# A shorter ring of per-expert buffers: six epack buffers become four in the routed expert stage

## What is computed

```python
x = _layernorm(x + attn(x))
aff = x @ centroids.T
assign = argmax(aff); alpha = sigmoid(aff of the chosen expert)
for e in range(8):                       # y of each token by its own expert alone
    h = relu(_layernorm(xs, ln_g[e], ln_b[e]) @ w1[e].T + b1[e])
    ye = xs + h @ w2[e].T + b2[e]
out = alpha * y + (1 - alpha) * xs
x = _layernorm(x + out)
```

## Time and profile before

| | |
|---|---|
| median of three runs | 863.51 us |
| profiled execution | 863.51 us, span 861.7 us |
| TensorE busy in the span | 837.3 us (97%) |
| VectorE, ScalarE, GpSimd busy | 456.1, 354.5, 282.1 us |
| mean granted TensorE clock | 0.994 |
| chain that ended last | TensorE 85%, VectorE 7%, DMA 2%, SyncE's stream 2% |
| moved by DMA | 93.29 MB, mean 108 GB/s |

### The profile page before, as it was taken

One profiled execution on the slowest core, in us unless ns is written; L12 is line 12 of the kernel. 1 busy time (PEld: TensorE's weight loads), 2 busy tenths in 40 slices (PEclk: granted clock), 3 DMA queues, 4 the chain that ended last, 5 costly groups with the idle time before them and its releaser, 6 DMA issues.

```text
span 861.7 us, 19429 instructions
## 1 busy us (share of the span) xinstructions
PE 837.3 (97%) x7394; PEld 559.6 (65%) x7394; DVE 456.1 (53%) x1334; ACT 354.5 (41%) x591; POOL 282.1 (33%) x392
## 2 busy tenths in 40 slices
PE   8999999999999999999999999999999899999994
PEld 5545576477466557557547646769988676767673
DVE  5465355256256346445528625624687465555552
ACT  1443425523532531631542453323232467565660
POOL 3503021422152060152142225224554444444422
PEclk9999999999999999999999999999999999999998
DMA  6501100020020020010003103333544897988830
GB/s 246 184 2 30 46 2 1 26 75 1 26 75 1 26 74 2 26 41 34 2 27 123 32 19 102 134 135 121 178 151 136 297 344 273 319 303 286 294 121 15
DMA packets 38594, 93.29 MB, mean 108 GB/s; under 512 B 13988, under 2 KB 26917, under 8 KB 30567
## 3 DMA queue, kind: packets, MB, share of 16 engines
q1 hardware_dynamic: 33206, 80.42, 26.4%
q0 software_dynamic: 4864, 11.10, 4.3%
q10 hardware_dynamic: 432, 0.54, 0.2%
HBM read 81.07 MB, written 11.23 MB: 107 GB/s over the span
## 4 chain that ended last, share of the span: by engine, by line
PE 85%; DVE 7%; DMA 2%; issue 2%; SPq 2%; ACT 1%; another core or an unknown queue 0%; POOL 0%; DVEq 0%; POOLq 0%; ACTq 0%
PE ps L598 13%; PE ps L604 12%; PE ps L545 9%; PE ps L569 7%; PE ps L691 7%; PE ps L709 6%; PE ps L731 4%; PE ps L755 4%; PE ps L517 3%; PE ps L577 3%; PE ps L444 3%; PE ps L465 3%; PE ps L473 3%; PE ps L407 2%; DMA wts<-in_w 1%
## 5 line engine op out<-in xcount | busy, mean ns | idle before, releaser
L604 PE MATMUL ps<-ff2T,hT 128*128 128x256 f32 x512 | 121.0, 384 | 0.2 <-ACT hT L1523 0.2
L598 PE MATMUL ps<-x3x,ff1T 128*128 128x512 f32 x256 | 118.8, 604 | 0.1
L1531 ACT ACTIVATE arena<-ps 128x1536 f32<-128x1536 f32 (+3 forms) x49 | 65.1, 1328 | 128.3 <-DVE arena L998 127.8
L604 PEld LDWEIGHTS ps<-ff2T,hT 128*128 128x128 f32 x512 | 94.3, 190 | 16.3 <-issue 3.4
L998 DVE SCALAR_TENSOR_TENSOR arena<-ps,arena 128x512 f32<-128x512 f32 (+4 forms) x59 | 44.9, 767 | 106.4 <-PE ps L545 64.0
L709 PE MATMUL ps<-w_sb,arena 128*128 x400 | 95.6, 382 | 0.0
L709 PEld LDWEIGHTS ps<-w_sb,arena 128*128 128x128 f32 x400 | 72.2, 190 | 16.0 <-issue 8.2
L598 PEld LDWEIGHTS ps<-x3x,ff1T 128*128 128x128 f32 x256 | 45.6, 190 | 52.2 <-issue 49.9
L545 PE MATMUL ps<-arena 32*128 32x512 f32 (+7 forms) x896 | 73.0, 434 | 1.8 <-ACT hT L1017 1.2
L545 PEld LDWEIGHTS ps<-arena 32*128 32x128 f32 x896 | 36.0, 184 | 37.2 <-issue 31.0
L1523 ACT ACTIVATE hT<-ps,col 128x512 f32<-128x512 f32 x64 | 43.8, 685 | 35.7 <-PE ps L598 35.1
(11 more groups left out here) (231 smaller groups left out, 1584.7 us busy)
## 6 DMA issues: line engine op xcount, KB each, us to landing
arena<-in_w SPq DMA_DIRECT2D x27, 1024.0 KB
hT<-in_w SPq DMA_DIRECT2D x16, 1024.0 KB
wts<-in_w SPq DMA_DIRECT2D x9, 1024.0 KB
w_sb<-in_w SPq DMA_DIRECT2D x8, 1024.0 KB, 5.1
token_store<-x SPq DMA_DIRECT2D x8, 520.0 KB, 3.7
arena<-in_x SPq DMA_DIRECT2D x8, 512.0 KB, 3.8
arena<-in_epack SPq DMA_DIRECT2D x18, 134.0 KB
slot_table<-padid POOLq DMA_DIRECT2D x4, 576.0 KB
```

The lines of the kernel that those rows point to most:

```text
L598: last = eng.matmul(ps[:, 6 + m % 2, :], ff1T[:, kd, m * P:(m + 1) * P], xT3[:, kd, :], start=kd == 0, stop=kd == KD - 1)
L604: last = eng.matmul(quarter(6, t), hT[:, m, t * P:(t + 1) * P], ff2T[:, m, :], start=m == 0, stop=m == FM - 1)
L1531: eng.activation(o, i, ACT.Relu).then_inc(s_sa, 1)
```

## The change

EN becomes 4. The tensor `ep_more` goes, all four buffers are those in the arena, and the four epack loads ahead of the loop are counted by EN instead of WN (both are 4). The wait in `slot_sp_ep` is not edited, but its index changes with EN: it now names the tile four before instead of six.

```diff
-UN, WN, XN, EN = 3, 4, 6, 6
+UN, WN, XN, EN = 3, 4, 6, 4
...
-        ep_more = sb("ep_more", [P, 2, EW + 12 * (NP - 1)])
...
-        ep = ring(at, EW + 12 * (NP - 1), EN - 2) + [ep_more[:, u, :] for u in range(2)]
-        at += (EN - 2) * (EW + 12 * (NP - 1))
+        ep = ring(at, EW + 12 * (NP - 1), EN)
+        at += EN * (EW + 12 * (NP - 1))
...
-                    for j in range(WN):
+                    for j in range(EN):
                         slot_sp_ep(eng, j, slot_sp_rows(eng, j))
```

## The result

The changed kernel takes 884.0 us (median of 4 runs, 883.1 to 886.4) against 863.6 for the kernel before on the same chip: ratio 1.0245, 95% interval 1.0219 to 1.0271, 20 us slower. The profiled execution took 882.1 us, with a span of 879.9.

What follows compares the result with a forecast made beforehand. TensorE, busy 147.6 of 150 us in the expert stage, was taken as the bound, with SyncE's load queue nearly late. Tile 14's 1.9, mixed tiles' 14.7 and tile 32's 1.5 sum to 18.1; 863.5+18.1 = 881.6, stated as 881, range 868 to 893.

Steps and rivals of the forecast that it cites:

- One of my own signs of being wrong: Whole run: the prediction is wrong if the granted clock falls more than once or twice more.
- Where the wait binds: SyncE's epack loads: tile j now waits for y(j-4); tiles 13, 21 and 28 go 1.8 to 8.0 us later.
- Tiles 4 to 12, nothing: Full tiles with one weight block each: weights and ids still arrive in time, so no cost.
- Tile 14, +1.9: Tile 13's held epack delays tile 14's blocks; TensorE's 2.37 us stall becomes 4.3, half clock already paid.
- The loop: Mixed tiles, y(j-4) to y(j-2): reaction 0.2, issues 5.7, ids 9.8, gather to y 3.1; 18.8 us, longer than two tiles.
- the 14.7: Mixed tiles: loop excesses 5.1, 7.6 and 6.2 us, less 1.4 hidden per run, leave 3.7+6.2+4.8 = 14.7.
- the hidden time: VectorE's lag: 1.4 us costs nothing, once per run of mixed tiles, until TensorE's turn at line 741.
- Tile 32, +1.5: Last mixed tile, no ids behind it: weights come 16.9 us after y28, wanted after 15.4, so +1.5 us.
- Rival (a): Ids overtake the weights, only the weights loop is left: 871.0 us; chance 0.14.
- (b): Rival, hidden: bursts land faster, loop below 16 us, only part of tile 14 costs: 863.5 to 865; chance 0.07.
- (c): Rival, faster: held SyncE clears the queue ahead of tile 14, stall and half clock go: 859.3 us; chance 0.04.
- (d): Rival: every new stall also halves the clock, 1.8 us each for eight more tiles, 881+14 = 895; chance 0.10.

Runs made afterwards that it cites:

- mixed-only run: Kernel before, six buffers, with the epack's wait for y(j-4) only at the nine mixed tiles, y(j-6) at full tiles: 880.3 us, ratio 1.0206.
- full-only run: Kernel before, six buffers, with the epack's wait for y(j-4) only at the full tiles, y(j-6) at mixed tiles: ratio 1.0040.
- second set: The second of three sets of follow-up measurements; the kernel before had a median of 860.1 us in it.
- five-buffer kernel: Kernel before with EN = 5, one of the two buffers in ep_more left unused: ratio 0.9998.
- ids experiment: Changed kernel, four buffers; from tile 14 on SyncE issues the ids of tile j+3 ahead of tile j's epack and weights: 870.7 us, ratio 1.0092.

## Why the prediction was right

**Forecast 881 us, measured 884.0.** The profiled execution took 882.1 against my sum of 881.6. That the two are so near is partly luck: several terms were off and cancelled, as below. One of my own signs of being wrong came too: I allowed the granted clock to fall once or twice more, and it falls three times more.

**Where the wait binds**: right. From tile 4 on the epack leaves 0.2 us after y(j-4), except where SyncE is later: at 22 of 30 tiles. I wrote some twenty such waits; eighteen are in the view.

**Tiles 4 to 12, nothing**: right, within 0.2 us up to y11.

**Tile 14, +1.9**: right by its size (y13 is 2.0 late, gap 4.10 for the 4.3 forecast) and its cause: the gap is gone but for 0.73 us in the mixed-only run, whose time is 4 us lower, and alone in the full-only run. Inside it two errors cancelled. The third block left 3.9 us later (676.07 for 672.16, since SyncE issued the blocks more slowly too), not 1.9, and TensorE started on it 9.3 us after its issue, not 11.3. The step took the half clock as paid already. That held in the traces compared; on the chip of the second set the five-buffer kernel had none, and tile 14 cost 3.5.

**The loop**: right. 18.8 forecast; 18.6, 18.5 and 18.7 measured at tiles 21, 23 and 25. Its terms were 0.2, 5.7, 9.8 and 3.1, and at tile 21 they are 0.2, 6.3, 9.0 and 3.1, so two were off by 0.6 and 0.8 in opposite senses; over all seven turns they are 6.3 and 9.2 on the mean. The ids experiment shows that this loop and not the weights carries the loss, though the gaps in the view stand at the weights: what ends a gap last is not what set its length. The excess of the loop, from y12 to y16, y17 to y23 and y24 to y28, was 5.3, 7.0 and 6.3 us for the 5.1, 7.6 and 6.2 forecast. But the runs of mixed tiles cost 5.0, 5.1 and 5.2 for 3.7, 6.2 and 4.8, so what was hidden or won back was 0.3, 1.9 and 1.1 us, not 1.4 each time. That the sum, 15.3, comes near to the 14.7 is luck in this part. Nor does TensorE stand where I had the hidden time end: at the transposes of the rows (line 741) it waits 0.3 us; what it stands more is at layer 1.

**Tile 32, +1.5**: 0.9 measured.

**Rival (a)**, ids overtaking the weights: fell. Ids issued behind three blocks started their gather 9.0 us later at tile 21, and 8.1 to 10.0 at all seven. **(b)** fell: no turn of the loop took under 18.5 us, for its 16. **(c)** fell: tile 14's gap grew. **(d)**, the clock halving at each stall: in part. The granted clock drops behind tiles 14, 18, 23 and 30, and TensorE is busy 4.6 us more, for the 14 that it named. Yet the time of the loop forecast holds without a term for it. That a slower TensorE inside a loop of SyncE, DMA, GpSimd and VectorE only fills time it would have stood is my reading; no run took the clock away.

## What to carry to other kernels

A ring's length isn't only a question of whether its own tiles arrive in time. Where one queue issues everything in order, the wait for a free buffer holds all that follows, so close the loop by hand: from the event waited for through every load behind it back to that event, against the time that the ring leaves; below it costs nothing, above it costs the excess at each turn (none at five buffers, 2.5% at four, 18% for a wait three tiles back). If such a wait must be shortened, move the large, early loads ahead of it first, and keep a small load that an engine needs soon off the back of a burst.

## What the runs showed of the hardware

TensorE's clock behind a gap of about two microseconds can go either way. At tile 14 it stood 2.37 us and its next matmuls took 1.08 us (1.2 GHz), and in another kernel, with the same work up to there, it stood 2.05 us and they took 0.63 (2.4 GHz); behind 3.29 us they took 0.63 at first too. So a repair of such a gap can win the gap alone, or the half clock with it. The executions of one kernel differ as well: on the chip of the second set the kernel before took 859.6 to 860.3 us fourteen times and 861.7 to 862.5 six times, some 2 us apart, near the 1.8 us that the half clock costs behind tile 14. That this is the same thing is likely but not shown, as there is no trace of them.

A small load issued behind three blocks of 1 MB comes late: in the changed kernel GpSimd's gather started 8.1 to 10.0 us after the ids behind them were issued, at all seven tiles.
